# A fourth tile of attention features, the values' product in slot 5, and the last three V products in one visit

## What is computed

```python
h = _layernorm(x) * (1 + ca) + sa
q, k, v = split(h @ qkv_w.T + qkv_b)      # 16 heads of 8
q, k = apply_rope(q), apply_rope(k)
attn = softmax(where(mask, -1e9, q @ k.T / sqrt(8)))
x = x + ga * ((attn @ v) @ proj_w.T + proj_b)
h = _layernorm(x) * (1 + cb) + sb
y = square(relu(h @ W_fc.T)) @ W_proj.T
x = x + gb * spikes(y)                    # five steps of a leaky threshold, counted, / 5
```

## Time and profile before

| | us |
|---|---|
| median of 3 runs | 444.27 |
| lowest and highest of them | 440.36, 444.50 |
| the profiled execution | 443.15 |
| its span, first to last instruction | 441.4 |
| TensorE busy in the span | 390.9 (89%) |
| VectorE busy | 329.3 (75%) |
| ScalarE busy | 256.8 (58%) |

### The profile page before, as it was taken

The page is one execution under the profiler, slowest core; times in us unless marked ns, Lnnn a source line. Parts: engine busy times, 40 slices in busy tenths (PEclk is TensorE's granted clock), DMA queues, the critical chain, the costliest instruction groups (busy, mean ns, idle before and its releaser), DMA issues.

```text
span 441.4 us, 15622 instructions
## 1 busy us (share of the span) xinstructions
PE 390.9 (89%) x6599; PEld 253.1 (57%) x6599; DVE 329.3 (75%) x730; ACT 256.8 (58%) x447; POOL 126.1 (29%) x163
## 2 busy tenths in 40 slices
PE   2778899888999989998899999998998889988885
PEld 2327555555656755666457654765566646753653
DVE  6659995886886988878986997699866777541176
ACT  8203465565676756765666665766665457566523
POOL 6714310430343043503342234304330220040020
PEclk9989999999999999999999999999999899998999
DMA  7056363243314233242415251323233050011001
GB/s 214 22 161 169 99 218 88 70 116 102 104 45 119 75 101 93 80 122 49 137 50 139 64 138 48 117 72 99 67 113 86 16 146 6 25 45 27 3 1 49
DMA packets 26050, 38.53 MB, mean 87 GB/s; under 512 B 5796, under 2 KB 20716, under 8 KB 23692
## 3 DMA queue, kind: packets, MB, share of 16 engines
q1 hardware_dynamic: 25980, 37.53, 29.8%
HBM read 26.35 MB, written 8.65 MB: 79 GB/s over the span
## 4 chain that ended last, share of the span: by engine, by line
PE 41%; DMA 18%; DVE 13%; ACT 10%; POOL 6%; issue 5%; SPq 5%; ACTq 0%; POOLq 0%; DVEq 0%
PE o_bank L611 10%; DMA kf<-k_scr 9%; PE d_bank L528 7%; DVE negmax L978 6%; PE t_bank L593 6%; PE s_bank L548 5%; DMA rden<-r_scr 4%; ACT probs L827 4%; PE a_bank L528 3%; DMA r_scr<-rden_c 2%; POOL parts L1303 2%; PE s_bank L528 2%; SPq L440 2%; PE t_bank L528 2%; POOL o_n L1325 2%
## 5 line engine op out<-in xcount | busy, mean ns | idle before, releaser
L978 DVE TENSOR_REDUCE negmax<-s_bank 128x1 f32<-128x512 f32 (+7 forms) x368 | 192.9, 566 | 56.9 <-PE s_bank L554 54.6
L827 ACT ACTIVATE probs<-t_bank 128x512 f32<-128x512 f32 x288 | 163.0, 594 | 89.8 <-PE t_bank L598 84.5
L548 PE MATMUL s_bank<-kf,qf 126*64 126x512 bf16 (+7 forms) x1024 | 118.7, 293 | 11.8 <-DMA kf<-k_scr 6.2
L593 PE MATMUL t_bank<-qf,kf 128*64 128x512 bf16 (+7 forms) x1024 | 113.3, 290 | 10.8 <-ACT probs L827 9.8
L611 PE MATMUL o_bank<-probs,v 128*32 128x512 f32 (+7 forms) x1024 | 75.1, 412 | 0.0
L548 PEld LDWEIGHTS s_bank<-kf,qf 126*64 126x64 bf16 x1024 | 50.6, 111 | 40.6 <-DVE negmax L978 19.9
L554 PE MATMUL s_bank<-causal,identb 128*64 128x64 bf16 x1024 | 72.6, 195 | 0.0
L598 PE MATMUL t_bank<-causal_t,identb 128*64 128x64 bf16 x1024 | 64.8, 195 | 0.0
L593 PEld LDWEIGHTS t_bank<-qf,kf 128*64 128x64 bf16 x1024 | 41.4, 110 | 35.1 <-ACT probs L827 14.4
L598 PEld LDWEIGHTS t_bank<-causal_t,identb 128*64 128x64 bf16 x1024 | 48.1, 111 | 9.3 <-issue 0.2
L554 PEld LDWEIGHTS s_bank<-causal,identb 128*64 128x64 bf16 x1024 | 47.1, 112 | 8.3 <-issue 8.1
(11 more groups left out here) (145 smaller groups left out, 455.9 us busy)
## 6 DMA issues: line engine op xcount, KB each, us to landing
qf<-q_scr SPq DMA_DIRECT2D x15, 576.0 KB
kf<-k_scr SPq DMA_DIRECT2D x45, 192.0 KB
q_scr<-parts SPq DMA_DIRECT2D x24, 128.0 KB, 1.7
k_scr<-parts SPq DMA_DIRECT2D x24, 128.0 KB, 1.7
xa<-in_x SPq DMA_DIRECT2D x8, 256.0 KB, 3.9
o_t<-o_raw SPq DMA_DIRECT2D x60, 32.0 KB, 2.4
rden<-r_scr SPq DMA_DIRECT2D x15, 128.0 KB
out_y<-count SPq DMA_DIRECT2D x7, 256.0 KB, 6.7
```

Source lines behind the costliest of these rows:

```text
L548: nc.tensor.matmul(bank[C * a:C * (a + 1), col:col + keys], qf[0:KS, slot, 2 * p + a, C * i:C * (i + 1)], kf[0:KS, slot, 2 * p + a, 0:keys ...
L593: nc.tensor.matmul(bank[C * a:C * (a + 1), col:col + w], kf[0:KX, slot, 2 * p + a, C * kb:C * (kb + 1)], qf[0:KX, slot, 2 * p + a, C * kb: ...
L827: nc.scalar.activation(probs[:, v, :], t_bank[u % 2][:, :], ACT.Exp, scale=SCALE).then_inc(e_done, 1)
L978: last = nc.vector.tensor_reduce(own[:, i, p:p + len(same)], cols, AX.X, ALU.max, negate=True)
```

## The change

The ring gets a fourth tile. To make room, buffers are laid over others: `rest` over `rot_s`, `sq` over `relu`, the modulation weights over `relu`, the row of ones over `count`. Two more clears of a tile are made by ScalarE at the start. The values' product moves from slot 0 to slot 5, its copy out of PSUM from slot 1 to slot 6, V blocks 3, 5 and 4 go together in slot 1, the projection from slot 16 to 17. The order of the rows in a feature tile is another: the repeated dimension of the query copy is now its outermost, and each of the three key copies now takes one part j and repeats it. So the keys of parts 0 and 1 can be spread before part 2 is stored, and the queue does that: at the end of batch b come the queries of half 2b+4 and two of its key copies, and the third follows the store of part 2.

```diff
-RING = 3
+RING = 4
-PV_LATE = {0: (3, 5), 1: (4,)}
+PV_LATE = {1: (3, 5, 4)}
-A_AT = {-16: T1, -13: QK, -9: QK + 1, 0: V_}
-D_AT = {16: PROJ, 25: T2, 27: FC, 29: FC + 1, 31: FC + 2, 33: FC + 3}
+A_AT = {-16: T1, -13: QK, -9: QK + 1, 5: V_}
+D_AT = {17: PROJ, 25: T2, 27: FC, 29: FC + 1, 31: FC + 2, 33: FC + 3}
...
+        rest = rot_s
...
+        sq = relu
+        wmod_sb = relu[:, 0:2, :].rearrange("p i c -> p (i c)")[:, 0:6 * P]
+        ones_row = count[0:MR, 0, 0:SEQ // 2].bitcast(BF16)
...
                 sp.dma_start(qf[0:FR, n % RING, own],
-                             q_rows.unsqueeze(1).to_broadcast([NPART * HD, NPART, many, SEQ])).then_inc(done, 16)
+                             q_rows.unsqueeze(0).to_broadcast([NPART, NPART * HD, many, SEQ])).then_inc(done, 16)
-            def spread_keys(n, own=slice(0, HH), done=None):
+            def spread_keys(n, own=slice(0, HH), done=None, some=None):
...
-                sp.wait_ge(k_stored, 16 * Q_STORES * (b + 1))
-                k_rows = k_scr[b % 2].rearrange("j (d h) c -> d j h c", h=H)[:, :, heads]
                 m = HD * NPART
-                for i in range(NPART):
-                    sp.dma_start(kf[m * i:m * (i + 1), n % RING, own], k_rows).then_inc(done, 16)
+                first, last = (0, NPART) if some is None else some
+                sp.wait_ge(k_stored, 16 * (Q_STORES * b + (2 if last < NPART else Q_STORES)))
+                for j in range(first, last):
+                    k_rows = k_scr[b % 2, j].rearrange("(d h) c -> d h c", h=H)[:, heads]
+                    sp.dma_start(kf[m * j:m * (j + 1), n % RING, own],
+                                 k_rows.unsqueeze(0).to_broadcast([NPART, HD, many, SEQ])).then_inc(done, 16)
...
                 if 0 < b < final:
                     store_part(b + 1, 1, 2)
-                if 0 < b < final:
-                    spread(2 * b + 2)
+                    spread_keys(2 * b + 2, some=(2, NPART))
...
                 if b + 2 < NB:
                     store_part(b + 2, 1, 1)
+                    spread_queries(2 * b + 4)
+                    spread_keys(2 * b + 4, some=(0, 2))
...
             place_values(0)
+            clear(3, qf)
+            clear(3, kf)
...
-                if at == 1 and 0 < b < final:
+                if at == 6 and 0 < b < final:
                     place_values(b + 1)
...
-                reach(dve, whole_done, 2 * (b - 1) + qk + 1)
+                reach(dve, whole_done if step == 0 else split_done, 2 * (b - 1) + qk + 1)
...
-                    if at == (8 if b == final else 10):
+                    if at == (8 if b == final else 9):
                         reciprocals(b - 1, 1)
-                    if at == 18:
+                    if at == (18 if b == final else 19):
                         residual1(b - 1)
```

More of the change, by code:

```diff
@@ L181, in adaln_kernel @@
         ct_sb = sb("ct_sb", [P, NB])
-        wmod_sb = sb("wmod_sb", [P, 6 * P])
         cos_sb = sb("cos_sb", [P, SEQ])
@@ L188, in adaln_kernel @@
         causal_t = sb("causal_t", [P, P], BF16)
-        ones_row = sb("ones_row", [MR, SEQ], BF16)
         minus_half = sb("minus_half", [P, NT])
@@ L212, in adaln_kernel @@
         whole = sb("whole", [P, 2, SEQ])
-        rest = sb("rest", [P, 2, SEQ])
+        rest = rot_s
         parts = sb("parts", [P, 2, NPART, SEQ], BF16)
@@ L241, in adaln_kernel @@
         relu = sb("relu", [P, NF, SEQ])
-        sq = sb("sq", [P, NF, SEQ])
+        sq = relu
+        wmod_sb = relu[:, 0:2, :].rearrange("p i c -> p (i c)")[:, 0:6 * P]
         count = sb("count", [P, 2, SEQ])
+        ones_row = count[0:MR, 0, 0:SEQ // 2].bitcast(BF16)
         y_sb = count[:, 1, :].rearrange("p (t d) -> p t d", d=D)
@@ L409, in spread_queries @@
                 sp.dma_start(qf[0:FR, n % RING, own],
-                             q_rows.unsqueeze(1).to_broadcast([NPART * HD, NPART, many, SEQ])).then_inc(done, 16)
-            def spread_keys(n, own=slice(0, HH), done=None):
+                             q_rows.unsqueeze(0).to_broadcast([NPART, NPART * HD, many, SEQ])).then_inc(done, 16)
+            def spread_keys(n, own=slice(0, HH), done=None, some=None):
                 b, half = divmod(n, 2)
                 heads = slice(HH * half + own.start, HH * half + own.stop)
+                many = own.stop - own.start
                 done = done or feat[n % RING]
-                sp.wait_ge(k_stored, 16 * Q_STORES * (b + 1))
-                k_rows = k_scr[b % 2].rearrange("j (d h) c -> d j h c", h=H)[:, :, heads]
                 m = HD * NPART
-                for i in range(NPART):
-                    sp.dma_start(kf[m * i:m * (i + 1), n % RING, own], k_rows).then_inc(done, 16)
+                first, last = (0, NPART) if some is None else some
[4 more added lines that the diff above has]
+                                 k_rows.unsqueeze(0).to_broadcast([NPART, HD, many, SEQ])).then_inc(done, 16)
             def spread(n, *some):
@@ L466, in _ @@
             sp.wait_ge(ones_made, 1)
-            sp.wait_ge(zeros_made[2], 2)
+            for slot in (2, 3):
+                sp.wait_ge(zeros_made[slot], 2)
             sp.dma_start(kf[KS:KX].rearrange("r s h c -> r (s h) c"),
```

## The result

| | before | after |
|---|---|---|
| median, us | 443.42 | 585.09 |
| lowest and highest | 440.36, 444.50 | 583.44, 587.77 |
| span of the profiled execution | 441.4 | 586.0 |
| its mean granted clock of TensorE | 0.988 | 0.866 |

The ratio is 1.322, with a 95% interval of 1.313 to 1.330. Forecast were 573 us and 520 to 680.

A forecast was written before the change was run, and what follows sets the result against it. The kernel was taken as bound by TensorE's own work, in batches of 46.8 us. 441.4 + 102 (six periods) + 29 (start) - 1 (small edits) = 571 us of span, and 1.75 around it: 573 us, range 520 to 680.

The forecast's parts named there:

- The number of engines: In the feature loads: query and key copies with outermost dimension 3 use three DMA engines, in place of 12 and 8.
- The price of an engine: In a feature load: 24.4 GB/s per engine, 74 GB/s for three, 52 at the other end; a load takes 18.5 us.
- rival (a): Three engines in the feature loads, but at the crowded price of 17.4 GB/s: 673 us; chance 0.15 for 640 to 720.
- The period: One batch: 63.8 us in place of 46.8, with 3.0 for the clock; six of them add 102 us.
- Odd chain: From the release in slot 9 to that in slot 27, load behind the maxima: 26.7 us, a wait of 6 to 7.
- Even chain: From slot 27 to the next slot 9, part 2's store behind early copies: 34.1 us, before 25.7; waits about 8.5.
- Start and end: First loads are late, slot 27 goes on at about 109 us, +29 us; the 79.6 us behind half 15 stay.
- The clock: On TensorE after each new wait: 3.4 us doing half the work, about 1.5 us lost, twice a batch, 3.0.
- The outputs behind the store: In SyncE's queue: outputs of half 2b-1, held by the wait for part 2, still come before the projection; that hides.
- rival (c): Engines stay 12 and 8, but key part 2 lands behind queries and two key copies: 438 or 443 us; chance 0.05.
- The small edits: Merged V blocks, moved values' product, two clears and overlaid buffers: together -1 us.
- The other signs: In the profile after: TensorE's key waits 80 to 110 us, SyncE's store wait some 10 per batch, clock below 0.95.

The follow-up runs named there:

- filled kernel: The changed kernel with six more TensorE products ahead of the wait for features in every half from 3 on: 570.48 us.
- kernel with eight engines: The changed kernel, queue order, fourth tile and slots kept, with feature copies rewritten to an outermost dimension of 8: 454.04 us, ratio 1.026 against the kernel before.

## Why the prediction was right

**The number of engines.** Right. Three engines, seen as a share of 0.19 in after and in the kernel with the order of rows alone; that kernel shows it to be cause enough for the whole loss. The rule of the Trainium skill cited in the prediction (DMA: Bandwidth & Descriptors, "Why a DMA increments its semaphore by 16 and not by 1") is borne out on dimensions of 3, 8 and 24, with shares of 0.19, 0.48 and 0.76.

**The price of an engine.** 24.4 GB/s was taken and 26.7 measured; the crowded end of 17.4, rival (a), is out. A load took 309.41 - 291.26 = 18.2 us from issue to use where 18.5 was forecast. That the two agree so well is in part luck. At 80 GB/s the bytes take 14.7 us, not 16.0, and with the 2.5 us put for issue and landing the sum would have been 17.2; what comes on top of the bytes took 3.4 us, not 2.5, and the two errors cancel in part.

**The period.** Odd chain: 309.41 - 280.95 = 28.5 us against 26.7 + 1.5. Even chain: 345.86 - 309.41 = 36.5 against 34.1 + 1.5. Together 64.9 against 63.8. The third key copy took 5.66 us from issue to landing where 0.7 + 2.6 + 1.3 = 4.6 had been put, again 1 us more. From the issue of the store of part 1 to the landing of part 2 went 340.14 - 324.15 = 16.0 us where 0.4 + 0.8 + 13.3 + 1.7 = 16.2 had been put. Over six periods the difference is 8 us with the first of them, which was 66.4.

**Start and end.** Slot 27 of the first batch went on at 112.8, forecast 109. The stage with slot 9 of half 0 was 6 us later than forecast, 86.8 against 81. Of these, 2.5 us had come before: the keys of half 2 were issued at 73.09, where the sum has 81 - 10.4 = 70.6. Behind them the copy of the second maxima had to land (the 13.5 us above), a transfer that the sum left out. So is the next one in the queue, the gates' rows (`rows<-g_scr`, 1536 KB, issued at 76.04); while it ran, the share of busy DMA engines was 0.8 to 1.0. Which of the two held TensorE how long was not separated. From 86.8 to 112.8 went 26.0 us where 28.2 had been put, which took back a part. Behind half 15 went 82.5 us, not 80; TensorE's clock was 0.50 in the first 3.4 us of it. Start, periods and end are 4, 8 and 3 us over, together the 15 by which the span of 586.0 exceeds the 571 forecast.

**The clock.** Forecast 1.5 us a wait from one stretch in the start. The filled kernel gets back 14.6 / 9 = 1.6 us for each fall of the clock that it prevents, and its chains without a fall, 34.4 and 26.7 us, are the 34.1 and 26.7 of the prediction. Right, in kind and size.

**The outputs behind the store.** The prediction said that their delay hides. In after it does, since slot 9 waits for the keys anyway: nearly all of VectorE's 66.8 us for the sums lies inside TensorE's waits. In the batch shown VectorE goes on at 347.17, 1.3 us after TensorE, which is busy throughout these 1.3 us. The kernel with the order of rows alone says the same, with 2.6 us of this wait and the same time. In rival (c) the same delay was put at 5 us of loss or less, 438 or 443 us. The kernel with eight engines is the nearest to it, though its queries run on 8 engines and not on 12, and it gave 454. The rival let the held outputs delay only the projection; the run shows VectorE's 21.8 us of waits for the sums in slot 9. TensorE's waits for keys are as the rival had them: of the 11.6 us one wait of 5.5 stands in the second batch, with the old queue order too (5.6), and the other six are 0.4 to 1.7 us each. How the loss divides between these two waits stays open.

**The small edits.** Put at -1 us together with the fourth tile's gain inside the loads. On a kernel that isn't paced by loads they were worth -3.1 us for the slots, and -5.8 with the tile. The prediction's split (2 us for fewer visits, up to 5.7 for the projection) was not tested part by part.

**The other signs.** TensorE's wait for the keys was put at 80 to 110 us and is 113.1. SyncE's wait for the store of part 2 was put at some 10 us a batch; in the six periods this store landed 11.4 to 14.7 us after its issue. The period is 65.1 us on average against 64, the granted clock 0.866 where under 0.95 was forecast.

Not tried: the new queue order with the store of part 2 put ahead of the early key copies, and the row order with 12 engines for the queries and keys by part.

## What to carry to other kernels

Before rewriting a copy, look at the outermost dimension of both sides: a repeat or a split of three put in front leaves three DMA engines at work, and nothing in the program's bytes shows it; the share of busy DMA engines in a window of the profile does. Ahead of a wait in a queue that issues everything, count what stands behind it and on which engine's work order it lands. Before a wait on the path is cured, look which one is next in line: the fourth tile alone took 5.3 us out of one wait, 4.7 came back in two others, and the time stayed.

## What was not expected of the hardware

SyncE's issue of a DMA took long in places where loads on three engines were outstanding. In the start of after, its queue in order of time (start, issue time):

```profile
37.91 7.36 SPq L392 DMA_DIRECT2D xa<-in_x  x1
45.31 9.17 SPq L482 DMA_DIRECT2D g_scr<-gate_t  x1
```

The same two issues took 0.57 and 0.47 us before. They stand behind the loads of half 0 and 1; the queue went on at 54.53, just before the features of half 1 let TensorE go at 57.87. In the batches the issue of the four copies of the sums behind an odd load took 5.91 us where it takes 2.68. The kernel with the order of rows alone shows the same in its start, with 4.92 and 9.42 us for these two issues. What limit is reached there no run told apart.
